# A GRU and expert kernel: the broadcast of a group's expert weights as eight transfers instead of one

## What is computed

```python
def reference(x, cond_1024, ...):
    def _L0_cond_ref(x, context, ...):                  # x: (2, 1024, 256)
        mixed = jnp.tanh(jnp.einsum('bte,he->bth', x, W_in) + b_in + ctx)
        h1 = _gru_layer(mixed, Wih0, Whh0, bih0, bhh0)
        h2 = _gru_layer(h1, Wih1, Whh1, bih1, bhh1)
        gate = jax.nn.sigmoid(jnp.einsum('bh,gh->bg', context, W_gate) + b_gate)
        gated = gate[:, None, :] * h2 + h2
        return jnp.einsum('bth,eh->bte', gated, W_out) + b_out
    def _L1_cond_ref(x, t_emb, ...):                    # 8 experts, 2 chosen
        shared = jax.nn.silu(xf @ w1) * (xf @ w3) @ w2
        s = jax.nn.sigmoid((jnp.concatenate([xf, tf], axis=-1) @ router_W).astype(jnp.float32))
        _, topk_idx = jax.lax.top_k(s + router_bias, K)
        ...
        combine = jnp.zeros((N, E), x.dtype).at[jnp.arange(N)[:, None], topk_idx].add(gates)
        h = jax.nn.gelu(jnp.einsum('nc,ech->enh', xf, W1e), approximate=False)
        y = jnp.einsum('enh,ehc->enc', h, W2e)
        routed = jnp.einsum('ne,enc->nc', combine, y)
        return ((shared + routed) / (N_SHARED + K)).reshape(Bb, Tt, C)
    x = x + _L0_cond_ref(x, cond_1024, ...)
    x = x + _L1_cond_ref(x, cond_1024, ...)
    return x
```

## Time and profile before

| | us |
|---|---|
| median of 3 runs | 2200.1 |
| lowest, highest | 2197.22, 2202.41 |
| the profiled execution, time | 2187.96 |
| the profiled execution, span | 2186.2 |
| PE busy | 2067.1 (95%) |
| PEld busy | 1481.8 (68%) |
| DVE busy | 1850.2 (85%) |
| ACT busy | 1198.9 (55%) |
| POOL busy | 561.6 (26%) |

### The profile page before, as it was taken

The page is one execution under the profiler, slowest core; times in us unless marked ns, Lnnn a source line. Parts: engine busy times, 40 slices in busy tenths (PEclk is TensorE's granted clock), DMA queues, the critical chain, the costliest instruction groups (busy, mean ns, idle before and its releaser), DMA issues.

```text
span 2186.2 us, 162053 instructions
## 1 busy us (share of the span) xinstructions
PE 2067.1 (95%) x69920; PEld 1481.8 (68%) x69920; DVE 1850.2 (85%) x11225; ACT 1198.9 (55%) x6471; POOL 561.6 (26%) x2542
## 2 busy tenths in 40 slices
PE   6999899999999999999999999999999999999987
PEld 4666666677676776667766676666767676778766
DVE  4888888888898888988889888888889888888874
ACT  2555555555555555555555555555555555555542
POOL 1222232222222223222232222222232222222220
PEclk9999999999999999999999999999999999999999
DMA  5000000000000000000000000000000000000000
GB/s 219 5 4 5 4 5 5 24 5 5 10 5 24 5 5 10 5 24 5 5 10 5 24 5 9 5 24 5 5 10 5 24 5 10 4 22 9 5 16 19
DMA packets 10879, 32.76 MB, mean 15 GB/s; under 512 B 1368, under 2 KB 6832, under 8 KB 9136
## 3 DMA queue, kind: packets, MB, share of 16 engines
q1 hardware_dynamic: 10160, 22.38, 2.8%
HBM read 20.22 MB, written 2.16 MB: 10 GB/s over the span
## 4 chain that ended last, share of the span: by engine, by line
PE 54%; DVE 30%; ACT 12%; issue 3%; DMA 1%; SPq 0%; POOL 0%; DVEq 0%; POOLq 0%
PE bank L337 25%; PE bank L329 16%; DVE n_first L408 10%; PE bank L276 10%; DVE cells L428 8%; ACT factors L476 7%; ACT cells L480 5%; DVE r_pre L399 4%; DVE z_pre L409 4%; PE bank L310 2%; DVE bank L417 1%; DVE n_second L384 1%; DVE x L691 0%; DVE bank L380 0%; DMA x_t<-in_x_t 0%
## 5 line engine op out<-in xcount | busy, mean ns | idle before, releaser
L337 PE MATMUL bank<-w_h,cells 128*22 128x128 f32 (+4 forms) x32768 | 1361.1, 281 | 21.9 <-DVE cells L428 13.3
L337 PEld LDWEIGHTS bank<-w_h,cells 128*22 128x22 f32 (+4 forms) x32768 | 851.8, 110 | 129.2 <-DVE cells L428 92.0
L329 PEld LDWEIGHTS bank<-w_h,cells 128*2 128x2 f32 (+15 forms) x28112 | 509.9, 113 | 528.2 <-DVE cells L428 504.2
L521 POOL TENSOR_SCALAR cells<-cells 128x4 f32<-128x4 f32 x2048 | 463.7, 226 | 1523.3 <-DVE cells L428 1521.5
L329 PE MATMUL bank<-w_h,cells 128*2 128x64 f32 (+15 forms) x28112 | 767.9, 225 | 78.1 <-DVE cells L428 54.6
L470 ACT ACTIVATE n_second<-r_pre 128x4 f32<-128x4 f32 x2048 | 426.2, 208 | 501.4 <-DVE r_pre L399 461.1
L476 ACT ACTIVATE factors<-z_pre 128x4 f32<-128x4 f32 x2048 | 429.7, 210 | 445.3 <-DVE z_pre L409 370.1
L408 DVE STREAM_TRANSPOSE n_first<-bank 128x64 f32<-128x64 f32 x2048 | 599.7, 293 | 29.1 <-PE bank L337 20.9
L428 DVE TENSOR_TENSOR_SCAN cells<-factors,cells 128x18 f32<-128x18 f32 x2048 | 398.2, 194 | 232.2 <-ACT cells L480 158.8
L399 DVE STREAM_TRANSPOSE r_pre<-bank 128x64 f32<-128x64 f32 x2048 | 481.9, 235 | 35.9 <-PE bank L329 26.6
L409 DVE STREAM_TRANSPOSE z_pre<-bank 128x64 f32<-128x64 f32 x2048 | 427.3, 209 | 0.0
(11 more groups left out here) (91 smaller groups left out, 560.8 us busy)
## 6 DMA issues: line engine op xcount, KB each, us to landing
c_all<-weights SPq DMA_DIRECT2D x6, 1024.0 KB
x_t<-in_x_t SPq DMA_DIRECT2D x4, 512.0 KB, 7.5
w_1e<-in_w_1e SPq DMA_DIRECT2D x1, 2048.0 KB
w_2e<-in_w_2e SPq DMA_DIRECT2D x1, 2048.0 KB
w_x<-in_w_x SPq DMA_DIRECT2D x2, 768.0 KB, 8.1
w_h<-in_w_h SPq DMA_DIRECT2D x2, 768.0 KB, 9.9
w<-in_w SPq DMA_DIRECT2D x3, 512.0 KB
out_y<-y SPq DMA_DIRECT2D x6, 256.0 KB, 2.6
```

The lines of the kernel that those rows point to most:

```text
L329: mm = pe.matmul(r_sums[l][p][32 * g:32 * g + B * (j + 1)], state_tile(l, j, kt), w_h[l][:, kt, g, 2 * U:], start=False, stop=False, tile_ ...
L337: mm = pe.matmul(sums[l][p][32 * g:32 * g + B * (j + 1), 0:width], state_tile(l, j, kt), w_h[l][:, kt, g, 0:width], start=False, stop=Fals ...
L521: pool.tensor_scalar(cell_part(step_rows(l, j), 3), cell_part(step_rows(l, j), 1), 0.5, None, ALU.mult)\
```

## The change

The spread of a group becomes eight transfers, one for each expert, 128 KB each for 256 tokens. Each is written in the slot after the one before it (in the last group all in the same slot), and waits until its predecessor has landed. They count on a semaphore `s_spread` of their own, which is never cleared; so `spread` leaves the group's semaphore sets and their halves. The first `hid` of every expert waits for its own transfer. The planner takes expert e's weights as there 8 + 2e half slots after `comb_t` (before: 12 for all), and 12 in the last group as before.

```diff
-    def transfer(self, name, after, took):
-
-        self.when[name], self.engine[name], self.value[name] = self.when[after] + took, "spread", 32
-        self.signals[name] = after
+    def transfer(self, name, after, took, value):
+
+        self.when[name], self.engine[name], self.value[name] = self.when[after] + took, "spread", value
...
-        late = [k for k, o in enumerate(mine) if any(self.half(w) != half for w in o[2])]
+        late = [k for k, o in enumerate(mine) if any(self.half(w) != half for w in o[2] if self.engine[w] != "spread")]
...
-                spread = m_sets[mix.half("spread")]["spread"]
                 if m == mix.when["comb_t"] // 2:
                     wait_for(sp, mix, "comb_t")
-                    sp.dma_start(weights[:, 0:n], comb_t[0:E, 0:n]).then_inc(spread, 16)
-                if m == mix.when["comb_t"] // 2 + 1:
-                    sp.wait_ge(spread, 16)
-                    sp.dma_start(c_all[:, :, 0:n], weights[:, 0:n].partition_broadcast(P)).then_inc(spread, 16)
+                    sp.dma_start(weights[:, 0:n], comb_t[0:E, 0:n]).then_inc(s_spread, 16)
+                for e in range(E):
+                    if m == mix.when["comb_t"] // 2 + 1 + (e if mix is not mixtures[-1] else 0):
+                        sp.wait_ge(s_spread, mix.value[f"spread{e}"] - 16)
+                        sp.dma_start(c_all[:, e, 0:n], weights[e, 0:n].partition_broadcast(P)).then_inc(s_spread, 16)
...
         def wait_for(eng, mix, name):
-            eng.wait_ge(m_sets[mix.half(name)][mix.engine[name]], mix.value[name])
+            if mix.engine[name] == "spread":
+                eng.wait_ge(s_spread, mix.value[name])
+            else:
+                eng.wait_ge(m_sets[mix.half(name)][mix.engine[name]], mix.value[name])
...
-                            mix.add("dve", f"hid{u}_{m}{q}", (f"act{u}_{m if LAST else KT - 1}", f"down{u - 2}") + (("spread",) if i == m == q == 0 else ()),
+                            mix.add("dve", f"hid{u}_{m}{q}", (f"act{u}_{m if LAST else KT - 1}", f"down{u - 2}") + ((f"spread{i}",) if m == q == 0 else ()),
...
-            mix.transfer("spread", "comb_t", 12)
+            spread_before = 16 * (1 + E) * mixtures.index(mix)
+            for e in range(E):
+                mix.transfer(f"spread{e}", "comb_t", 8 + 2 * e if mix is not mixtures[-1] else 12, spread_before + 16 * (e + 2))
```

More of the change, by code:

```diff
@@ L70, in __init__ @@
         self.ops = {k: [] for k in ("pe", "act", "dve")}
-        self.when, self.value, self.engine, self.signals, self.small = {}, {}, {}, {}, []
-    def transfer(self, name, after, took):
-        self.when[name], self.engine[name], self.value[name] = self.when[after] + took, "spread", 32
-        self.signals[name] = after
+        self.when, self.value, self.engine, self.small = {}, {}, {}, []
+    def transfer(self, name, after, took, value):
+        self.when[name], self.engine[name], self.value[name] = self.when[after] + took, "spread", value
     def add(self, engine, name, waits, issue, beside=False, small=False):
@@ L104, in half @@
     def half(self, name):
-        return self.when[self.signals.get(name, name)] // self.window
+        return self.when[name] // self.window
     def total(self, engine, half):
@@ L222, in gru_moe_kernel @@
         s_hist = sem("s_hist")
+        s_spread = sem("s_spread")
         KINDS = ("r", "pe", "turn", "for_n", "n", "for_h", "h", "pool", "bias", "x", "xn", "go")
         sets = [[{k: sem(f"s_{k}{l}_{p}") for k in KINDS} for p in range(2)] for l in range(2)]
-        m_sets = [{k: sem(f"m_{k}_{p}") for k in ("pe", "dve", "act", "spread", "out", "go")} for p in range(2)]
+        m_sets = [{k: sem(f"m_{k}_{p}") for k in ("pe", "dve", "act", "out", "go")} for p in range(2)]
         def numbers(semaphores):
```

## The result

The changed kernel takes 2210.02 us (median of 7, 2205.57 to 2214.03) against 2200.1 (median of 7, 2195.59 to 2207.88): ratio 1.004, 95% interval 1.0022 to 1.0058. It is slower by 9.9 us where 8.3 us of gain were forecast. Its profiled execution took 2210.09 us, its span is 2208.3.

The account below looks back on a forecast made before the run. The recurrence, a PE, DVE, ACT, DVE round trip per slot, was taken as the limit. Terms -11.5 + 2.8 + 0.5 + 0.2 - 0.3 = -8.3 us took 2200.1 to 2191.8 us, range 2185 to 2199.

Parts of the forecast that it names:

- Part 2: Last group's spread: eight 64 KB transfers in a row at 1.7 us each delay the last expert's product, +2.8 us.
- Part 1: Groups 0 to 5: splitting the 1 MB broadcast ends nearly all 12.1 us of PE's waits for instructions, -11.5 us.
- rival A: PE's stalls at the spreads have another cause than the broadcast and stay; +3.2 us, 2203.3 us, chance 0.10.
- rival C: Groups 0 to 7: each train starves PE a little at about four instruction packets; +7.1 us, 2207.2 us, chance 0.08.
- Part 3: On DVE, 63 more first products wait for `s_spread`, nearly hidden and none really waiting, +0.5 us.
- Part 4: Expert work moved to other half slots: +0.2 us in group 7, -0.3 us at the seam to the last group.
- the seam: Before the last group, work moved 4 half slots earlier leaves POOL's gating as the last to finish, -0.3 us.
- B: Last group's serial train costs 2.2 us per transfer, +6.8 in place of +2.8; sum -4.3, 2195.8 us, chance 0.19.
- pivot of 1.36 us each: Last group's spread: the time per transfer from which the serial train of eight begins to hurt.

Follow-up runs that it names:

- e4: Changed kernel with its moved instructions, added waits and own semaphore, but one transfer for all experts in every group; ratio to the kernel before 1.000 (0.9983 to 1.0018).
- f1: The changed kernel run again without an edit, on a chip with other variants; ratio to the kernel before 1.0035 (1.002 to 1.005).
- e9: Changed kernel, but in no group do the eight transfers wait for each other; ratio to the kernel before 0.9957 (0.9939 to 0.9974).
- g3: e9 run again unedited in another job; ratio to the kernel before 0.9963 (0.9953 to 0.9974).
- e6: Changed kernel, but the last group's eight transfers have own semaphores and do not wait for each other; ratio to the kernel before 0.9941 (0.9918 to 0.9964).
- f2: e6 run again unedited in another job; ratio to the kernel before 0.9979 (0.9965 to 0.9993).

## Why the prediction was wrong, point by point

- **The main places were the right ones, the sizes were not.** The terms were -11.5 for the middle's stalls and +2.8 for the last spread. They turned out near -4 to -8 (one job says -12) and at +13.2.
- **Part 2, the last group's spread: the step that failed.** The time of one transfer was put together as 0.97 + 0.23 + 0.49 = 1.7 us. The first and the last part were about right: the changed kernel's first transfer has 0.96 before its first packet and 0.4 behind its last. The middle part, an eighth of the bulk, was wrong: in the one transfer all 1024 packets of data start within 3.09 us, eight rows of DRAM being read side by side, and a transfer of one row reads it 128 times in a line, which takes 1.52 us and not 0.23. Measured 2.8 to 3.1 us, above both ends of my range (1.21 to 2.3), so +12.3 in place of +2.8. The upper end came from a load of different rows, and the change reads one. The Trainium skill's fixed cost ("DMA: Bandwidth & Descriptors", Anatomy of one DMA), with 2.15 us an estimate by that page, was nearer than mine but also short, and for the transfer of 128 different rows (1.81) too long; the page fits it on transfers issued from GpSimd, and these are issued from SP.
- **What was not thought of: the clock.** A PE that waits some 2.3 us for every expert drops to half clock (0.50 from 2190 to 2200 us); from the last expert product to `y` it took 0.9 us more.
- **Part 1, the stalls.** That a broadcast starves PE of instructions is shown: without most of the middle's broadcasts the kernel is 0.6% faster, on two chips, and the long stalls stand where two instruction packets are 5.4 us or more apart. The Trainium skill's round-robin rule (the same page, Queues, rings and completion order), rival A, did not carry the day: the stall is the broadcast's. But I took the first profile's 12.1 us as the size of it. Counted alike, that profile has 13.5 us, and the others of one transfer 6.6 to 11.4. And I left only 0.6 us for what a split keeps. It keeps most: 6.4 us of waits where one expert alone has 3.1. A train of some 22 us, in place of the 14 that I reckoned with, meets six instruction packets and not four. Whether PE also has less in store than I read out of 1.4 against 2.5 us is not shown. This is rival C's mechanism at well under half of its price of 16 us.
- **Part 3, more waits: 0.5 us.** e4 has them all and is at 1.000. No product in the middle waits for `c_all`: the trace has 8 such waits, all in the last group. Right within what can be told.
- **Part 4, moved instructions: +0.2 us.** Within what can be told, by e4. At the seam -0.3 was expected: from the last step of the recurrence to `comb_t` it is 12.92 us before, and in the 14 traces with the moved work 12.56 in seven (e4 and f1 among them) and 13.8 in the other seven, the changed kernel's own profile with 13.78 among them. In all 14 the work that used to fill the wait for POOL is gone and PE stands 2.06 us or so. What differs is the clock: in the seven longer ones 3.4 us at half clock fall between that step and `comb_t`, in the others none, so the mean is near +0.3. In the changed kernel the piece behind the wait got 0.55:

```profile
2166.56 1.71 PE L276 MATMUL bank<-hist,w_out 128*32 128x128 f32 x32 [2.06 <-POOL hist L539]
```

- **The rivals.** B, the dear train, was the right mechanism with a price of 6.8 where 13.2 was due. None of my cases had it at a size that turns the sign by itself, though its pivot of 1.36 us each stood in the text.

What stays open: without the middle's broadcasts the kernel gains 13 us, while the waits on issue fall by 7. The changed middle was measured at 0.16 to 0.54% by different jobs. And the middle of e9 and g3 gains about 0.4%, 9 us (their ends give nothing of it: from the last step to `y` 27.6 and 27.8 us, before 27.1), though their waits fell by 3.6 only, to 6.6 on average, like those of f1. So the count of waits is a part of the cost, and I can't say where the rest is.

What beats both kernels is eight transfers, each with a semaphore of its own, that do not wait for each other: in all groups (e9 and g3) 0.9957 and 0.9963 to before, in the last group alone (e6 and f2) 0.9941 and 0.9979. The mean is the same, the first pair agrees better; which of the two is faster is not shown.

## What to carry to other kernels

Splitting a transfer divides its bytes but not its time: here an eighth of what took 4.66 us took 2.9. A chain of parts that wait for each other belongs only where nobody waits for the last one. Give the parts semaphores of their own and let them be under way together. And look at the instruction queue when a long transfer runs beside a TensorE of many small instructions: the stall stands under "issue", varies from execution to execution (6.6 to 13.5 us here), and one profile is no measure of it. Neither is one comparison a measure of a gain of 0.3%: the same kernel differed by 0.38% between two chips.

## What the hardware showed that I had not expected

- 128 partitions that read one row of DRAM: 2.80 to 2.84 us for 512 B each, 2.51 for 64 B; 128 different rows of 512 B: 1.81 to 1.82; 32 partitions from one row 1.69, 8 partitions 1.57. The packets of one row start 12 ns apart (1.52 us for 128, 0.78 for 64, 0.39 for 32). Eight such broadcasts under way together started all their packets within 6.33 us.
- At 22 of 30 broadcasts of 1 MB in one transfer two instruction packets started 5.4 to 6.7 us apart, where one comes each 3.6 us, and PE waited 1.1 to 3.4 us on issue; at the other eight, with at most 4.9 us, it waited 0 to 1.2.
- The granted clock of TensorE fell to 0.50, the level of 1.2 GHz, while it worked for 6.38 of 10 us in pieces with waits between.
